# Causal latent attention in one layer: TensorE's written-out order found by a search over 128 plans, four sets of softmax weights, and diagonal key tiles spread among a chunk's others

## The reference

```python
att = jnp.einsum('bhql,bhkl->bhqk', q_for_k, k_lat) * L ** (-0.5)
att = jnp.where(causal[None, None], att, -jnp.inf)     # causal: key <= query
att = jax.nn.softmax(att, axis=-1)
y_lat = jnp.einsum('bhqk,bhkl->bhql', att, v_lat)
y = y_lat @ l2o_w.T + l2o_b
```

## Time and profile before

| | |
|---|---|
| median of 3 runs | 2953.5 us (2951.43 to 2960.58) |
| the profiled execution, its own time | 2953.24 us |
| its span, first to last instruction | 2951.5 us |
| mean granted TensorE clock | 0.968 of full |
| TensorE matmul (PE) busy | 2811.8 us, 95% |
| VectorE (DVE) busy | 2124.7 us, 72% |
| ScalarE (ACT) busy | 1828.5 us, 62% |
| GpSimd (POOL) busy | 803.5 us, 27% |

### The profile page before, as it was taken

How to read it: one execution, slowest core, us unless ns; L and a number is a source line. 1 busy time by engine, 2 the same in 40 slices (tenths; PEclk the granted TensorE clock), 3 DMA queues, 4 the chain that set the end, 5 groups by cost and what they waited for, 6 DMA issues and landing times. The chain is left out here.

```text
span 2951.5 us, 48579 instructions
## 1 busy us (share of the span) xinstructions
PE 2811.8 (95%) x16538; PEld 1915.6 (65%) x16538; DVE 2124.7 (72%) x5590; ACT 1828.5 (62%) x3673; POOL 803.5 (27%) x785
## 2 busy tenths in 40 slices
PE   8999989999999999999999999999979996999991
PEld 7888755555555655555555555555457774899991
DVE  7888788888888888888888888888334443545444
ACT  5666535766666676666666676666745453655554
POOL 7888620110110110111111011011025554122332
PEclk9999978999999999999999999999989998999995
DMA  7787852413332432432431432331053320434326
GB/s 227 265 286 265 290 130 55 106 43 88 91 91 75 95 83 70 109 80 59 108 96 43 94 82 63 88 82 32 5 166 121 108 83 24 120 74 105 78 25 236
DMA packets 259529, 320.32 MB, mean 109 GB/s; under 512 B 70563, under 2 KB 157644, under 8 KB 258001
## 3 DMA queue, kind: packets, MB, share of 16 engines
q1 hardware_dynamic: 241616, 294.02, 35.3%
q0 software_dynamic: 17664, 23.19, 3.9%
HBM read 182.69 MB, written 143.95 MB: 111 GB/s over the span
## 5 line engine op out<-in xcount | busy, mean ns | idle before, releaser
L941 ACT ACTIVATE att_probs<-att_score_bank 128x512 f32<-128x512 f32 (+3 forms) x2560 | 1159.0, 549 | 590.2 <-PE att_score_bank L867 582.3
L996 DVE TENSOR_REDUCE att_partial_max<-att_max_bank 128x1 f32<-128x512 f32 x1536 | 1004.9, 687 | 119.1 <-PE att_max_bank L855 113.6
L855 PE MATMUL att_max_bank<-att_k_st,att_q_st 96*128 96x512 f32 (+3 forms) x1792 | 642.2, 382 | 7.9 <-DVE att_partial_max L996 6.8
L867 PE MATMUL att_score_bank<-att_q_st,att_k_st 98*128 98x512 f32 (+3 forms) x1792 | 641.4, 384 | 2.4 <-ACT att_probs L941 2.3
L1000 DVE CUSTOM_DVE_ANT_0 att_edge_sum<-att_max_bank,first_edge 128x128 f32<-128x128 f32 (+3 forms) x1024 | 481.9, 483 | 150.9 <-PE att_max_bank L855 150.5
L883 PE MATMUL att_acc_bank<-att_probs,att_v_st 128*32 128x512 f32 (+3 forms) x5120 | 545.5, 539 | 1.4 <-POOL att_probs L980 0.9
L980 POOL TENSOR_SCALAR_AFFINE_SELECT att_probs<-att_probs 128x512 f32<-128x512 f32 x256 | 162.8, 636 | 1314.9 <-ACT att_probs L941 1314.9
L867 PEld LDWEIGHTS att_score_bank<-att_q_st,att_k_st 98*128 98x128 f32 x1792 | 334.2, 188 | 188.8 <-ACT att_probs L941 107.2
L855 PEld LDWEIGHTS att_max_bank<-att_k_st,att_q_st 96*128 96x128 f32 x1792 | 344.0, 193 | 149.3 <-DVE att_partial_max L996 74.7
L883 PEld LDWEIGHTS att_acc_bank<-att_probs,att_v_st 128*32 128x32 f32 x5120 | 132.1, 109 | 246.1 <-issue 135.8
L241 POOL TENSOR_TENSOR proj_op_low<-proj_turned,proj_op_high 128x512 fp32r<-128x512 f32 x192 | 244.2, 1295 | 47.0 <-ACT proj_op_high L401 44.8
(11 more groups left out here) (239 smaller groups left out, 4466.7 us busy)
## 6 DMA issues: line engine op xcount, KB each, us to landing
qk_parts<-proj_parts SPq DMA_DIRECT2D x64, 1024.0 KB, 5.3
att_k_st<-qk_parts SPq DMA_DIRECT2D x168, 256.0 KB, 6.0
att_q_st<-qk_parts SPq DMA_DIRECT2D x159, 256.0 KB, 4.1
v_tokens<-proj_v_tok SPq DMA_DIRECT2D x64, 256.0 KB, 4.6
att_v_st<-v_tokens SPq DMA_DIRECT2D x64, 256.0 KB, 6.9
exp_w<-in_ew SPq DMA_DIRECT2D x16, 1024.0 KB, 8.2
first_q<-qk_parts SPq DMA_DIRECT2D x33, 256.0 KB, 3.9
dispatched<-att_empty_rows SPq DMA_DIRECT2D x8, 1036.0 KB, 4.1
```

The costliest lines, as they stand in the source:

```text
L855: nc.tensor.matmul(max_ps[u % MAXB][:, 0:width], q_tile(n)[0:3 * L, j, t * P:(t + 1) * P], k_tile(g, kb)[0:3 * L, j, 0:width], start=True, ...
L867: nc.tensor.matmul(score_ps[h % SCOREB][:, q0:CH], k_tile(g, kt // TT)[:, j, (kt % TT) * P:(kt % TT + 1) * P], q_tile(n)[:, j, q0:CH], sta ...
L941: nc.scalar.activation(probs[:, k % PROBS, j, q0:CH], score_ps[(HG * k + j) % SCOREB][:, q0:CH], ACT.Exp).then_inc(exped, 1)
L996: nc.vector.tensor_reduce(best, bank[:], AX.X, ALU.max).then_inc(unit_reduced, 1)
```

## The change

Three things change, all in the attention.

- `key_tiles(c)` gives the order of a chunk's key tiles: 0 first, then a diagonal tile, then c of the others, and so on. For c = 1 it is 0, 4, 1, 5, 2, 6, 3, 7; for c = 3 it is 0, 12, 1, 2, 3, 13, 4, 5, 6, 14, 7, 8, 9, 15, 10, 11. For c = 0 it stays 0, 1, 2, 3. The accumulation's stop flag follows the last step of the list.
- `PROBS` is 4 in place of 3.
- `Order` no longer takes the cheapest next kind. It holds up to 128 partial plans, extends each by each kind that may come next, keeps the one with the least due time among those with the same counts, and of these the 128 with the least due time. The due time is the plan's clock, plus the bare cost of all TensorE work left, plus 0.1 for each step still to be weighed. The costs are new: 0.082 to go into the tiled form of the array, 0.222 to go out of it, a weight load of 0.115 after a wait, and new ones for VectorE and ScalarE. There is no limit of two steps in a row. The time at which a chunk's rows are there is now VectorE's time plus 7.0, without a queue.

```diff
+def key_tiles(c):
+    tiles, left = [0], list(range(1, TT * c))
+    for edge in range(TT * c, TT * (c + 1)):
+        if edge:
+            tiles.append(edge)
+        tiles += left[:c]
+        left = left[c:]
+    return tiles + left
+
-KS = [(s, c, kt) for s in range(SLOTS) for c in range(NC) for kt in range(TT * (c + 1))]
+KS = [(s, c, kt) for s in range(SLOTS) for c in range(NC) for kt in key_tiles(c)]
-BURST = 2
-GATHER = 2
-EVEN = 0.1
-JOIN = 0.1
-PROBS = 3
+PROBS = 4
+MATMUL, TILED, INTO_TILES, OUT_OF_TILES, RELOAD, SIGNAL = 0.0218, 0.028, 0.082, 0.222, 0.115, 0.06
+DRAIN, ROWS_PUT, BURST_SHARE = 0.172, 7.0, 0.1
...
+    WIDTH, ALIKE = 128, 1
...
+    def weigh(self, plan):
+        k = plan.w
+        n = self.of_step[k]
+        free = plan.ready[0]
+        if KS[k][2] == 0 and n:
+            if plan.divided[0] < n - 1:
+                return None
+            free = max(free, plan.divided[1])
+        start = max(plan.now + INTO_TILES * (not plan.tiled),
+                    max(free + SIGNAL, plan.last) + (0.05 if plan.tiled else RELOAD))
...
+    def followers(self, plan):
+        u, h, w = plan.u, plan.h, plan.w
+        step = min(h, NS - 1) // HG
+        if u < NU and self.of_unit[u] - self.of_step[step] <= QBUF - 2:
+            yield self.unit(plan)
+        if h < NS and h // HG - PROBS < w:
+            yield self.score(plan)
+        if w < NK and plan.ready:
+            yield self.weigh(plan)
+        if plan.read is not None:
+            yield self.turn(plan)
+
+    def search(self):
...
+        for _ in range(NU + NS + NK + CHUNKS):
+            alike = {}
+            for plan in plans:
+                for p in self.followers(plan):
+                    if p is None:
+                        continue
+                    p.due = (p.now + self.units_left[p.u] + self.scores_left[p.h] + self.weighs_left[p.w]
+                             + BURST_SHARE * (NK - p.w) + OUT_OF_TILES * p.tiled + 0.5 * (CHUNKS - p.t))
+                    alike.setdefault((p.u, p.h, p.w, p.t, p.tiled), []).append(p)
+            plans = []
+            for group in alike.values():
+                group.sort(key=lambda p: p.due)
+                plans += group[:self.ALIKE]
+            plans.sort(key=lambda p: p.due)
+            plans = plans[:self.WIDTH]
+        self.note(plans[0])
...
-                                            stop=(kt == TT * (c + 1) - 1), skip_group_check=True)
+                                            stop=(k + 1 == LAST_STEP[n]), skip_group_check=True)
```

More of the change, by code:

```diff
@@ L12 @@
+import itertools
 from contextlib import ExitStack
@@ L576, in starts @@
[L576 to L582, removed]
-        if h < NS and h // HG - PROBS < w:
[L584 to L671, removed]
-        s, c, kt = KS[k]
-        if h % HG == HG - 1 and kt >= TT * c:
-            self.pool = max(self.pool, self.exped[h] + 0.1) + 0.64
-            self.masked[k] = self.pool + 0.05
-        self.h += 1
@@ new lines, in __init__, with unit @@
+        self.weighs_left = remaining(self.weigh_cost)
+        self.vector_extra, self.rows_after = {}, {}
+        for n, through in enumerate(UNITS_THROUGH):
+            for u, cost in ((through - 1, 0.13), (through, 0.08), (through + 1, 0.08), (through + 2, 0.13)):
+                self.vector_extra[u] = self.vector_extra.get(u, 0.0) + cost
+            self.rows_after[min(through + 2, NU - 1)] = n
+        self.search()
+    def unit(self, plan):
+        u = plan.u
+        start = max(plan.now + OUT_OF_TILES * plan.tiled, max(plan.reduced[0] + SIGNAL, plan.last) + RELOAD)
+        p = plan.copy()
+        p.kind, p.now, p.last, p.tiled, p.u = "unit", start + self.unit_cost[u], start, False, u + 1
+        drained = start + self.columns[u] / 2400 + DRAIN
+        if self.diagonal[u]:
+            vector = (drained + 0.192 if drained > p.vector else p.vector) + MASKED_MAX[self.columns[u]]
+        else:
+            vector = max(p.vector, drained + 0.038) + 0.598
+        p.reduced = p.reduced[1:] + (vector + 0.075,)
+        vector += self.vector_extra.get(u, 0.0)
+        if u in self.rows_after:
+            p.rows += ((self.rows_after[u], vector + ROWS_PUT),)
+        p.vector = vector
+        return p
@@ new lines, in score @@
+    def score(self, plan):
+        h, k = plan.h, plan.h // HG
+        free = plan.exped[0]
+        if h % HG == 0 and KS[k][2] == 0:
+            rows = [at for n, at in plan.rows if n == self.of_step[k]]
+            if not rows:
+                return None
+            free = max(free, rows[0])
+        start = max(plan.now + OUT_OF_TILES * plan.tiled, max(free + SIGNAL, plan.last) + RELOAD)
+        p = plan.copy()
+        p.kind, p.now, p.last, p.tiled, p.h = "score", start + self.score_cost[h], start, False, h + 1
+        n = self.queries[k]
+        drained = start + n / 2400 + DRAIN
+        slot_free = plan.weighed[k - plan.w]
+        p.scalar = max(drained + 0.06 if drained > p.scalar else p.scalar, slot_free) + n / 1185 + 0.046
+        exped = p.scalar + (0.1 if n > P else 0.16)
+        p.exped = p.exped[1:] + (exped,)
+        if h % HG == HG - 1:
+            if KS[k][2] >= TT * KS[k][1]:
+                p.pool = max(p.pool, exped + 0.1) + 0.64
+                exped = p.pool + 0.05
+            p.ready += (exped,)
+        return p
```

91 lines of the change are left out of this document (68 added, 23 removed).

## The result

The changed kernel takes 2902.86 us (median of 4 runs, 2902.28 to 2905.36) against 2952.47 us of the kernel before (4 runs): ratio 0.9828, 95% interval 0.9809 to 0.9847. The profiled execution took 2903.09 us with a span of 2901.3. Predicted were 2900. So the total is right to 3 us, but the sum behind it is not: the steady part gave less than predicted and the start much more.

The account below looks back on a forecast made before the run. TensorE's order was taken as the bound. Savings of 16.5 us switching and 20 us waits in ten slots made 52 over the steady part; with 3 for start and tail, 2953.2 became 2898, rounded to 2900, range 2868 to 2943.

Parts of the forecast that it names:

- What bounds the kernel: Attention's steady part: TensorE has 967 us of work in 1070 for ten slots; another order can win only the lost 103.
- The switching: TensorE's moves into and out of tiled weighings: 0.30 us a burst, 66 us in ten slots, 16.5 to be saved.
- N: Number of weighing bursts in ten slots of the steady part: 220 before, 165 forecast, bounds 100 and 200.
- The waits: TensorE's short waits for score banks, last exponentials and max banks: 37 us in ten slots, 17 left, saving 20.
- B: Queued work with which VectorE enters a burst: 1.2 us on average before, 1.6 assumed with three of four banks full.
- rival A: Steady part: VectorE's feeding sets the time and waits give back most of the gain; total 2930 to 2946, chance 0.20.
- Start and tail: Both ends of the attention stage: 3 us off together, bounds -15 and +10; the 5.88 us VectorE stall stays.
- Four sets: Fourth set of weights: a condition for third steps in a row, with no price of its own.
- Spreading: Diagonal key tiles set between wide ones: counted as 0, at the very most 12 us a slot lost.
- Rival C: Steady part: bursts of three and four starve VectorE and ScalarE, making the kernel slower, 2996 us; chance 0.08.
- Rival B: Steady part: the search does better, 130 bursts and waits below 10 us, total below 2868; chance 0.11.
- The marks named beforehand: Trace signs: 150 to 180 bursts in ten slots, slots of 103 to 104 us, VectorE's steady share 87 or 88%.

Follow-up runs that it names:

- e11: Changed kernel whose search is told that switching between tiled and plain work costs nothing: 2984.3 us, ratio 1.0095 to the kernel before.
- e12: Changed kernel with five sets of weights and a due time that favours earlier scores: 2891.0 us, ratio 0.9782 to the kernel before.
- e8: Changed kernel with three max banks and four score banks in place of four and three: 2952.8 us, ratio 0.9997 to the kernel before.
- e7: Changed kernel whose search keeps one plan in place of 128, units at most 120 ahead of scores: 2978.6 us, ratio 1.0086 to before.
- e10: Kernel before with GpSimd's memset moved early and chunk 4's load issued behind the put of chunk 1's rows: 2949.8 us, ratio 0.9980.
- e4: Kernel before, keeping its old step by step rule, given four sets of weights and spread key tiles: 2954.3 us, ratio 0.9999.
- e1: Changed kernel with three sets, the old key tile order and units at most 120 ahead of scores: 2915.6 us, ratio 0.9869 to before.
- e3: Changed kernel with key tiles back in their old order, four sets kept: 2908.5 us, ratio 0.9845 to the kernel before.
- e5: Kernel before with chunk 4's load issued at score 24 in place of 12, behind the put of chunk 1's rows: 2954.05 us, ratio 1.0000.
- e9: Kernel before with GpSimd's 6.92 us memset moved to its idle time around 380 us: 2955.2 us, ratio 1.0000.

## Why the prediction was right in the total and off in its terms

- *What bounds the kernel.* TensorE's order, with 967 us of work in ten slots, 66 of switching and 37 of waits: the cuts by equal work give 970, 63 and 39. Confirmed, and e11 confirms the price of a burst.
- *The switching.* N = 165 was taken, 195 came: 7 us saved in ten slots in place of 16.5. Mis-sized.
- *The waits.* 17 were taken, 26 came (from 39): 13 saved in place of 20. Mis-sized. For the steady part the two made 29.5 us out of the predicted 52.
- *B*, the queued work with which VectorE enters a burst, stands behind both, and it was the value put in that was too hopeful: 1.6 for 1.2. Solved from the same sum, 879 + 302 + (0.7 - B) N = 1051.8, the changed kernel has B = 1.36; e12 has 1.42, e8 with three max banks 1.11, before 1.2. That sum is only VectorE's balance of work and idle time, with B solved from the measured time, so it can't fail. For the same reason the prediction's 1071 us against 1070 measured, with which it supports the sum and rival A, was no test. What tests it is B read in the traces, as the mean time from a burst's start until VectorE has done what it had: 1.38 us before, 1.60 changed, 1.65 in e12, 1.25 in e8. It rose by 0.2 us, where 0.4 was taken. B alone does not make a good order: e7 has 1.60 too, but its bursts last 2.46 us on average against 1.63, and VectorE then idles 1.53 us a burst against 0.80.
- *Start and tail.* 3 us were taken off with bounds of -15 and +10; the start gave 18.8 and the tail -0.9, 17.9 together and outside the bounds. This step failed in its mechanism. It named the half clock and gave it no price, and 14.7 us came from there. It took the VectorE stall of 5.88 us as one "which stays", without asking what GpSimd did at that moment, and it read SP's queue as early everywhere, while chunk 1's rows stood behind a load; e10 prices these two at 5.7 us.
- *The total.* The steady part missed by -22.5 us, start and tail by +15, and 2.8 us came ahead of the stage and behind it, of which the prediction said nothing. The errors nearly cancel, so that the total is right to 3 us is in good part luck.
- *Four sets* were called a condition with no price of their own. e4 and e1 to e3 bear this out: nothing under the old rule, 7 to 10 us under the search. But the condition was wrong in its reason, that with three sets a third step leaves ScalarE nothing to write: e1 has three sets and 61 bursts of three steps in its steady part. The waits did not vanish with four sets, nor with five (20 us), as by the rule that the prediction draws from the Trainium skill, Perfetto Trace Analysis (Optimization Strategy), they might have. Its price for that rule is also wrong: the 17 us left are 24 us over the steady part, not 29. That the number of PSUM banks for the max units matters is shown by e8.
- *Spreading* was counted at 0 beside B; it gave 3 to 6 us. TensorE waits for no GpSimd select at L937 of the changed kernel, where it did twice before, for 0.9 us.
- *Rival A* (VectorE sets the time) did not come: its range was 2930 to 2946. What is right in it is that VectorE's share of a burst limits the order: the Trainium skill, TensorEngine Tiling (PSUM Bottleneck), says that draining may become the bound, and in e8, with one PSUM bank less to drain, the whole gain is lost. *Rival C* is e7; the 0.28 us "as now" in its working is 37/133, while the kernel before had 37/220 = 0.17. *Rival B* did not come.
- *The marks named beforehand.* 150 to 180 bursts: 195, of them 30% with three or four steps. A slot of 103 to 104: 105.2. VectorE's share to 87 or 88%: 85.2% (1293.06 of 1518.00), against 84.5%; by the prediction's own test this spoke against it, and rightly for the steady part. VectorE's idle time at a burst should be longer each and less in sum: 0.80 us against 0.76, 227 against 242 us in the steady part. The waits for a max bank should not grow: 38.4 us against 45.6, and 66 us both times with those for the masked reductions.

What was not settled: why the clock stays up in the start under the search, and how e12's gain is shared between the fifth set and the due time.

## What to carry to other kernels

When an order is searched rather than ruled, buffers and operand orders that did nothing before begin to pay; test them under the search, not under the old rule. Price a burst by what the engines that it starves have queued when it begins: longer bursts without looking ahead (e7) cost three times in waits what they save in switching. And when a stage's start differs, cut both traces at equal work, split the difference into work done at the lower clock and the rest, and look at every engine and queue at the stall: one cause can hide another, so that each undone alone shows nothing (e5, e9) and both together do (e10).

## What the runs showed of the hardware

A cast from SBUF to SBUF on VectorE waited for a GpSimd memset to end: 6.41 to 6.44 us in three kernels (before, e4, e5) where it began some 0.5 us behind a memset of 6.92 us, 5.61 us where it began 1.34 us behind (e8), and 0.17 us where none ran (e9, changed). The Trainium skill, SBUF — State Buffer (Who interferes with whom), says that a cast can take both of VectorE's port pairs, one of which it shares with GpSimd under an exclusive lock; the trace agrees. The same section says that a VectorE instruction with two inputs in SBUF contends with a GpSimd instruction that reads SBUF. In the changed kernel the subtraction behind the cast took 0.63 us while a select of 0.64 ran from 397.92, and in the kernel before, with GpSimd idle, 0.17, so the trace agrees here too:

```profile
397.95 0.63 DVE L1069 TENSOR_TENSOR att_max_parts<-att_neg_max,att_max_parts 128x16 fp32r<-128x16 f32 x1
```
